# A message-passing kernel: pacing 160 gathers, and unread products on TensorE

## The reference, cut to what matters

```
x = x + conv(group_norm(x))            # gates and scans over both axes, then a projection
t = t + attention(layer_norm(t))       # 16 batches, 256 tokens, 16 heads of 4 channels
t = t + ffn(layer_norm(t))             # graph attention picks 2 of 4 experts per node
```

```
e     = leaky_relu(a_src[src] + a_dst[dst], 0.2)
alpha = exp(e - max over edges of dst) / sum over edges of dst
agg   = sum over edges of dst of h[src] * alpha
```

## Time and profile before

| what | value |
|---|---|
| median of 3 runs | 957.09 us (947.78 to 957.43) |
| profiled execution | 955.78 us, of which the span is 954.2 us |
| PE busy | 623.1 us, 65% of the span |
| VectorE busy | 707.5 us, 74% |
| ScalarE busy | 415.9 us, 44% |
| POOL busy | 323.9 us, 34% |
| TensorE clock granted, mean | 0.791 of full |
| attention, first scores to last output | about 171 to 562 us |
| counting stage, first to last one-hot block | 594.2 to 851.8 us |

### The profile page before, as it was taken

The page is one execution under the profiler, slowest core; times in us unless marked ns, Lnnn a source line. Parts: engine busy times, 40 slices in busy tenths (PEclk is TensorE's granted clock), DMA queues, the critical chain, the costliest instruction groups (busy, mean ns, idle before and its releaser), DMA issues.

```text
span 954.2 us, 12789 instructions
## 1 busy us (share of the span) xinstructions
PE 623.1 (65%) x4576; PEld 309.0 (32%) x4576; DVE 707.5 (74%) x1465; ACT 415.9 (44%) x730; POOL 323.9 (34%) x384
## 2 busy tenths in 40 slices
PE   1504571479788888888878884495766857882421
PEld 1201140124344343444333443242333423352421
DVE  3699895886888887888888883175667475689966
ACT  2641351133455554555444467454562754412116
POOL 1000100016577675773000004575667555500000
PEclk9956675555799997999797995697888897997555
DMA  6000104000000000000000025110001011100001
GB/s 173 0 0 0 61 20 104 9 1 1 1 1 2 1 0 0 0 0 0 1 1 1 1 89 101 11 9 8 8 8 10 6 8 9 8 1 1 4 1 45
DMA packets 22010, 16.93 MB, mean 18 GB/s; under 512 B 13505, under 2 KB 18961, under 8 KB 21185
## 3 DMA queue, kind: packets, MB, share of 16 engines
q1 hardware_dynamic: 15440, 14.02, 5.4%
q0 software_dynamic: 5392, 2.18, 2.9%
q10 hardware_dynamic: 1120, 0.00, 0.1%
HBM read 10.51 MB, written 2.54 MB: 14 GB/s over the span
## 4 chain that ended last, share of the span: by engine, by line
DVE 40%; PE 30%; another core or an unknown queue 9%; ACT 7%; issue 3%; SPq 2%; DMA 0%; DVEq 0%; ACTq 0%
DVE mx L1372 11%; PE psum L617 9%; DVE arena L1454 8%; PE psum L775 6%; PE psum L672 3%; PE psum L633 3%; ACT arena L996 3%; SPq L408 2%; DVE arena L1108 2%; PE psum L648 2%; DVE arena L1104 2%; ACT arena L1078 2%; DVE mz L1391 1%; PE psum L659 1%
## 5 line engine op out<-in xcount | busy, mean ns | idle before, releaser
L1372 DVE TENSOR_REDUCE mx<-psum 128x2 f32<-128x512 f32 x256 | 164.2, 683 | 67.0 <-PE psum L633 65.7
L1454 DVE TENSOR_TENSOR arena<-arena,psum 128x4096 bf16<-128x4096 bf16 x64 | 143.7, 2283 | 92.4 <-remote 57.5
L502 POOL DMA_INDIRECT work<-node_rows,idx x160 | 156.2, 976 | 99.0 <-issue 46.7
L968 ACT ACTIVATE arena<-psum 128x1024 f32<-128x1024 f32 x128 | 130.9, 1023 | 115.4 <-PE psum L648 115.3
L617 PE MATMUL psum<-arena 128*32 128x256 f32 x1024 | 154.2, 427 | 1.0 <-ACT arena L976 0.5
L477 POOL TENSOR_SCALAR work<-arena,cF 128x184 f32<-128x184 f32 x128 | 93.3, 741 | 122.1 <-DVE arena L1246 64.4
L633 PE MATMUL psum<-arena 32*128 32x256 bf16 x512 | 83.0, 305 | 32.2 <-DVE mx L1372 20.2
L775 PE MATMUL psum<-arena 128*128 128x512 bf16 x256 | 69.7, 428 | 30.5 <-DVE arena L1454 29.7
L775 PE MATMUL psum<-arena,work 128*128 128x512 bf16 x256 | 66.3, 411 | 30.3 <-DVE arena L1454 30.2
L617 PEld LDWEIGHTS psum<-arena 128*32 128x32 f32 x1024 | 52.6, 118 | 64.9 <-issue 38.7
L479 POOL TENSOR_TENSOR work<-work,arena 128x368 f32<-128x368 f32 x64 | 61.8, 965 | 5.3
(11 more groups left out here) (318 smaller groups left out, 1007.3 us busy)
## 6 DMA issues: line engine op xcount, KB each, us to landing
work<-work SPq DMA_DIRECT2D x48, 64.0 KB, 2.0
work<-node_rows,idx POOLq DMA_INDIRECT x160
arena<-in_L_ffn_edge_index_dram SPq DMA_DIRECT2D x2, 1024.0 KB, 13.3
work<-edge_nodes SPq DMA_DIRECT2D x4, 368.0 KB
digits<-arena SPq DMA_DIRECT2D x1, 1024.0 KB, 3.9
arena<-digits SPq DMA_DIRECT2D x1, 1024.0 KB, 4.8
arena<-in_jpat_dram SPq DMA_DIRECT2D x1, 1024.0 KB, 7.2
out_dram<-work SPq DMA_DIRECT2D x4, 256.0 KB, 2.3
```

The lines of the kernel that those rows point to most:

```text
L502: pool.indirect_dma_start(gath[:, l, :], None, tab, bass.IndirectOffsetOnAxis(ap=idx[:, l:l + 1], axis=0)).then_inc(done, 16)
L968: act.activation(pbuf[:, n % 4, :, :, :], ps[:, 2 + 2 * (n % 2):4 + 2 * (n % 2), :].rearrange("p j (k q) -> p j k q", k=U), ACT.Exp).then_ ...
L1372: v.reduce_max(mx[:, h, :], ps[:, h % 2, :].rearrange("p (u k) -> p u k", u=U), AX.X).then_inc(mx_done, 1)
L1454: v.tensor_tensor(oh[:, buf, 0:HB, :], jp, pdig[:, here].rearrange("p (j c) -> p j c", j=1).broadcast_to([P, HB, HC]), ALU.is_equal).then_ ...
```

## The change

It has two parts.

1. **Gathers.** There are now four semaphores `gathered[0..3]`, and gather l adds 16 to number l % 4. Before it is issued, POOL waits until that semaphore holds 16 * (l // 4), that is, until gather l - 4 has landed. The waits for one-hot blocks are gone. Those who read the rows wait for all four semaphores: 4 * 92 each (23 gathers of 16) for the first half, 4 * 160 (40 gathers of 16) for the second.
2. **Unread products.** A new function `keep_busy(bank, n)` on TensorE multiplies the 128x128 identity by 512 columns of a constant into a PSUM bank, n times; nobody reads the result. It is called ahead of the products of `scores_t` (one product), in `turn_maxima` before its wait (six) and in `turn_slots` before its last wait (ten). The first two only where the batch number is an int, so in the bodies outside the hardware loop; `turn_maxima` also only while more batches follow.

```diff
-        gathered = (sem("first_half_gathered"), sem("second_half_gathered"))
+        gathered = [sem(f"gathered_{n}") for n in range(4)]
...
-            def gather(first, last, done):
-
-                for l in range(first, last):
-                    if l < USUAL and 2 * l // 5 - 7 > 0:
-                        pool.wait_ge(h_ready, 2 * l // 5 - 7)
-                    pool.indirect_dma_start(gath[:, l, :], None, tab, bass.IndirectOffsetOnAxis(ap=idx[:, l:l + 1], axis=0)).then_inc(done, 16)
+            def gather():
+
+                for l in range(USUAL):
+                    n, before = l % 4, l // 4
+                    if before:
+                        pool.wait_ge(gathered[n], 16 * before)
+                    pool.indirect_dma_start(gath[:, l, :], None, tab, bass.IndirectOffsetOnAxis(ap=idx[:, l:l + 1], axis=0)).then_inc(gathered[n], 16)
...
-            gather(0, LT, gathered[0])
-            gather(LT, USUAL, gathered[1])
+            gather()
             with pool.If(longer > 0):
-                gather(USUAL, CAP, rest_gathered)
+                for l in range(USUAL, CAP):
+                    pool.indirect_dma_start(gath[:, l, :], None, tab, bass.IndirectOffsetOnAxis(ap=idx[:, l:l + 1], axis=0)).then_inc(rest_gathered, 16)
...
+            def keep_busy(bank, n):
+
+                for _ in range(n):
+                    pe.matmul(ps[:, bank, :], identb, cB[:, 0:CH], start=True, stop=True)
+
             def scores_t(i, buf, m):
...
+                if isinstance(i, int):
+                    keep_busy(3 + 2 * (m % 2), 1)
...
             def turn_maxima(i, more):

+                if more and isinstance(i, int):
+                    keep_busy(7, 6)
                 pe.wait_ge(mz_ready, i + 1)
...
                 mm.then_inc(slots_turned, 1)
+                pe.wait_ge(qke_ready, 4 * (B - 3) + 4)
+                keep_busy(7, 10)
                 pe.wait_ge(cand_copied, 1)
...
             def turn(t):

-                pe.wait_ge(gathered[t], 16 * (LT, USUAL - LT)[t])
+                for n in range(4):
+                    pe.wait_ge(gathered[n], 4 * (LT, USUAL)[t])
...
             def list_maxima(t):

-                v.wait_ge(gathered[t], 16 * (LT, USUAL - LT)[t])
+                for n in range(4):
+                    v.wait_ge(gathered[n], 4 * (LT, USUAL)[t])
```

## The result

The kernel after took 1043.75 us (median of 4 runs, 1042.2 to 1044.48), the kernel before beside it 952.43 (median of 4, 946.68 to 957.43). The ratio is 1.096, 95% interval 1.088 to 1.104. The forecast was 959, the range 900 to 1000; the time lies 44 us above its top. The profiled run took 1043.4 us with a span of 1041.2.

What follows compares the result with a forecast made beforehand. Counting was held by TensorE's signals reaching VectorE late while gathers stream, attention by TensorE at its lower clock, VectorE nearly so elsewhere. 955.8 + 12 (gathers) - 8.9 (products) = 959 us; range 900 to 1000, the forecast's own 940 to 980.

Steps and rivals of the forecast that it cites:

- The wait for landing costs nothing: Gathers: waiting for gather l-4 costs 0, since a gather lands about 2 us after its issue.
- POOL streams at 1.25 us without a pause, until about 790: Counting stage: 160 gathers from 583.76 reach 784, up to 6 us more for collisions, instead of ending at 831.3.
- Under the stream VectorE gets a block through in 5.5 us; bounds 3.88 and 12.3: Counting stage: 34 blocks in 185 us of stream, 36 with the first two; 28 remain.
- these stretches are a stream without a pause, as after the change: Reason for taking 5.5 us a block: stretches late in earlier bursts showed blocks in 5.6 and 5.15 us.
- the slow bound: Counting stage: two blocks in 24.6 us, as in the first burst; 47 left at 790, end at 914, +62 us.
- After the stream 2.63 us a block: Counting stage: the 28 blocks left after the gathers take 74 us, the last ending at 864.
- The stage: Counting stage as a whole: last block ends at 864 instead of 851.8, +12 us; bounds -25 and +62.
- The products raise the clock: Attention stage: dense unread products lift TensorE's clock, batches go to VectorE's bound; sum -8.9 us, bounds -12 and +10.
- The clock doesn't rise, as by the rule: Rival, attention stage: products bring only their price, +10 us, time 978; chance 0.06.
- The stream starves the counts: Rival, counting stage: without POOL's pauses blocks take 8 us or worse, +41 to +62, time 988 to 1009; chance 0.17.
- Limited gathers cure the stall: Rival, counting stage: four gathers in flight end the late signals, -45 to -89 us, time 858 to 903; chance 0.25.
- The pace is indifferent: Rival, counting stage: the stall belongs to the counting itself, gathers change 0, time 947; chance 0.08.

Runs made afterwards that it cites:

- e4: Kernel after with its products, but POOL waits for nothing between gathers, neither for blocks nor for landings; 1052.27 us.
- e14: Kernel after with a POOL fill of 192 columns behind each gather; 1000.87 us (median of 2), ratio 1.047 to the kernel before.
- e13: Kernel after with a POOL fill of 288 columns behind each gather; 903.28 us (median of 4), ratio 0.947 to the kernel before.
- e1: Kernel before with the unread products alone, gathers and their waits for blocks unchanged; 942.71 us (median of 5), ratio 0.989.
- e5: Kernel after, but each gather waits for the one two places in front to land; 1044.65 us.
- e7: Kernel after with a POOL fill of 576 columns behind each gather, up to four gathers in flight; 934.15 us.
- e3: Kernel after, but each gather waits for the one directly in front to land; 1104.21 us.
- e11: Kernel after, but POOL's 160 DMAs are plain transfers of rows by position, four in flight at most; 867.62 us.
- e8: Kernel after, but SyncE issues 160 plain transfers of rows by position instead of POOL's gathers; 856.83 us.

## Why the prediction was wrong

**What the traces say together.** Take it that each gather needs about 1.40 us of something behind POOL that TensorE's products need too, and that POOL can issue one every 1.25 us. Then 0.15 us of work piles up with each gather. TensorE is free again when the pile is gone: number of gathers x 1.40 after the first issue. The kernel before: 25 gathers in the first burst, from 583.76; 583.76 + 35.0 = 618.8, and VectorE got on at 618.88. The second burst, 20 gathers from 621.44: 649.4, and VectorE got on at 649.90. A later one, 20 gathers from 683.75: 711.8, and VectorE got on at 712.34. The kernel after: 567.73 + 160 x 1.40 = 791.7; the last stalled block starts at 791.06. e4: 570.09 + 224 = 794.1; 794.67. The 2.80 is twice the 1.40, and each product of TensorE has a weight load of its own (4678 of each on the page).

So the account gives the moment at which a stall ends. It doesn't give all. The pile can't be rows still to be moved: POOL's wait for the gather four places in front cost 4.3 us in all, so they landed in pace, and from 780 to 791 us the DMA engines' share was 0.00. It doesn't say when the hold sets in, some 25 us into the stream of the kernel after. And e14 speaks against it: at a step of 1.39 the pile would grow by 0.01 us with each gather, and its average over all 160 gathers is 1.44, yet VectorE waited 100.3 us without a named releaser; e13's average is 1.52. It is shown that a hold exists, that it goes by the step, and that the kind of transfer (indirect, of scattered rows) makes it. What the shared thing is stays open, and the pile is argued.

**Step by step.**

- *The wait for landing costs nothing.* Right: 4.3 us in 2 waits, and e4 shows that it isn't the cause of anything.
- *POOL streams at 1.25 us without a pause, until about 790.* Right in length: 204.6 us, predicted 200 to 206. The end is 772.4, since the start was 16 us earlier.
- *Under the stream VectorE gets a block through in 5.5 us; bounds 3.88 and 12.3.* This is the step that failed. 10 blocks had started when the gathers ended, not 36. From 595.68 to 772.86 five blocks went, one in 35 us. The mistake was the sentence "these stretches are a stream without a pause, as after the change". The two stretches of the earlier trace rows begin 13 and 10 us into bursts of gathers, from 714.89 and from 787.12, each behind a pause of POOL (4.84 and 2.47 us) in which the pile, in the account above, had been worked off. They show how the stream begins, not how it is once it stands. The kernel after has the same easy start: six blocks in its first 30 us. Even the slow bound was too low, since its 24.6 us for two blocks came from a burst that POOL's own wait had cut off.
- *After the stream 2.63 us a block.* Nearly: 2.79. But 19 us passed between the end of the gathers and the end of the stall, which had no term in the sum.
- *The stage:* +12 predicted, bounds -25 and +62, measured +103 (360.7 for 257.6 us).
- *The products raise the clock.* Right. By the intervals from mark to mark: -2.2 for the predicted -1.4, -6.1 for -6.8, -1.0 for -0.9 up to the third mark (241.67 to 262.82), -3.6 for -2.0, -3.6 for -0.5 over the two intervals behind (477.49 to 520.65 against 491.34 to 538.09), +1.7 for the +2.1 of the tail. The start (190.02 for 191.21) and the stretches not named, each under half a microsecond, make up the rest. -8.9 predicted for the whole, -16 between these two traces, -12 by e1's timed runs.
- *The clock doesn't rise, as by the rule* (the Trainium skill, TensorE: Matmul & The Clock Gate, Part 1). The earlier trace rows have TensorE busy 84% of an interval at clock 0.50; here TensorE is busy 21.63 of 27.70 us, 78%, at a mean clock of 0.82. A smaller busy share has the higher clock, so busy time as the profile counts it isn't what decides; what differs between the two is the dense products. This rival fell.
- *The rivals.* "The stream starves the counts" had the right mechanism and sign, at 0.17. Its price, 8 us a block or worse up to the slow bound of 12.3, was at most a third of the 35 that came. The evidence for it stood in the prediction itself: the release came after POOL's stop each time. I read it as a delay that a block gets over in 5.5 us, where the delay grew with the stream: 35 us from the first of 25 gathers to the release, and 223 us from the first of 160. "Limited gathers cure the stall" fell as it was meant, by the number in flight: with two in flight it stays (e5), with four and a longer step it is gone (e7). One in flight does end it (e3), by a step of 2.86. "The pace is indifferent" fell with e7.

## What to carry to other kernels

Before you take a producer's brake away, ask what the brake was for. If an engine's waits have no named releaser while another engine streams, suspect the stream and take it away or slow it down once. If release times grow with the length of the burst, the price for an unbroken stream is not the average of short bursts. Divide the time from a burst's first issue to the release by the number of issues: here bursts of 25 and 20 gathers give 1.40 and 1.42 us, above the 1.25 of the step, and that could be had from the kernel before. A slower stream can be the faster kernel: 0.22 us more between two gathers took 140 us off this one (e13 against the kernel after).

## What the runs showed of the hardware

- Indirect DMAs (128 rows of 96 bytes each, from POOL) issued every 1.25 us let those who wait for TensorE see one product done in 2.80 us. At 1.39 the counting still stalls (100.3 us of VectorE's waits in e14), at 1.47 it hardly does (195 us for 64 blocks), at 1.55 and above it doesn't (178 us).
- 192 products of 16 columns took 5.1 us with no gather running, 7.3 to 7.4 at steps of 1.63 and 1.71 us, 10.9 at 1.55 and 32.1 at 1.47.
- Plain DMAs of the same size, of rows that lie together, did nothing to the counting: 160 within 107 us from POOL (e11), and SyncE's in e8 (177 us for the 64 blocks in both).
- The hold is in the profile only as gaps of 2.53 us put down to "issue" between single products, and as "remote" or "issue" in those who wait for TensorE. The records of eight counts stand there in 3.59 us, 64 us before the block that waits for them. It lasted up to 19 us beyond POOL's last gather, the last 11 of them (780 to 791 us) with no engine and no DMA engine busy.
- One gather in flight gave a step of 2.86 us on average.
- With unread dense products of 512 columns TensorE's granted clock was 0.82 for 0.50 and 1.00 for 0.67 in two intervals, and the kernel gained 1.1% from 102 of them (e1).
